# Making the scan's input product on GpSimd a batch ahead, and evicting the first expert block behind the decays

## The chip, the cores and the metric

The kernel runs on one core of a Trainium2 chip. The metric is the device time of one launch in microseconds (us). Inside a core, five engines with a queue of instructions each work side by side and wait for one another through semaphores: TensorE (PE, with its weight loads as PEld), VectorE (DVE), ScalarE (ACT), GpSimd (POOL) and SyncE (SP, which here issues nearly all the transfers). Each engine works through its own queue strictly in order, so that an instruction that waits holds up everything behind it on its engine.

## What is computed

The input is `x` of shape (8, 512, 128): 8 batches of 512 time steps. After a layer norm, a Mamba block `s` and a mixture-of-experts block `g` are computed, and the result is `x + s * g`. The Mamba block is the part that matters here:

```python
x_ssm = silu(conv(x_ssm) + conv_b)
dt = softplus(x_ssm @ dt_w + dt_b)
A = -exp(A_log); Bt = x_ssm @ Bp; Ct = x_ssm @ Cp
def step(state, inp):
    dA = exp(dt_t[:, :, None] * A[None])
    state = state * dA + (dt_t * x_t)[:, :, None] * B_t[:, None, :]
    y_t = einsum('bds,bs->bd', state, C_t)
...
y = (y + x_ssm * D) * silu(z);  s = x + y @ Wout
```

There are 256 channels and 64 states a channel. The product `dt_t * x_t` is what the kernel calls u. The experts (8 routed, of which 2 are chosen for a token, and 2 shared) are matmuls with a gelu between them.

## The kernel before

**Prologue.** For each batch `b` the kernel projects x and z, convolves, makes dt, u, B and C, and stores z (`sz_d`), x (`xs_d`), dt (`dt_d`), u (`u_d`), C (`c_d`) and parts of B. `dt_and_u(b)` on VectorE ends with `dt_new` and `u_new = dt_new * silu_x_new`; `store_dt(b)` on SP stores both, 512 KB each (256 channels of 512 float32). Meanwhile GpSimd sends the normalised tokens to their experts' places in DRAM by 64 indirect stores of 128 rows ("the scatters", line 675), two in flight. Only behind the last of them come its products of the scan phase. Near its end SP starts the scan phase's first loads: rows of C, broadcast to all partitions (`load_c`, 1 MB each), in two halves.

**Scan phase.** Each of 8 batches has 8 groups (`g`) of 8 states, so there are 64 groups, numbered `u = 8 b + g`, and a state step is two scans (`h` = 0, 1, the halves of the channels) over 512 times. In a group the engines do, for state `i`:

- ScalarE makes the decays exp(dt A) in `group_decay` (line 945), a group ahead of VectorE: its decays for group u wait for VectorE's scans of the same state in group u - 1, since they take their place. For kind E it also makes diagonals of B (line 952). Between them stand its evictions: `evict_block(u - 1)` at `i == 4` (line 888, it empties the expert block's bank), `copy_x_block(u)` at `i == 6` (line 894), and behind the eight states `hidden_tiles` with the gelus (lines 905, 913).
- The term u B comes in three kinds, `KIND`. D: PE broadcasts a row of B (line 1435) and VectorE multiplies it by u in PSUM (line 1222). E: PE makes it in `fill` (line 1449) by matmuls of the turned u with a diagonal, in two halves, with expert work between them. P, the last state of the groups with expert blocks: GpSimd multiplies u by a row of B (line 711, at `i == 1`), and ScalarE puts the decay into PSUM (line 939).
- VectorE scans (lines 1240 and 1230), GpSimd multiplies the states by C (line 703, `products`), and PE sums the products (line 1463). States have two buffers: scan `i` waits for product `i - 2`.

The first 40 groups (batches 0 to 4) run an expert block of 256 tokens each (`blocks`); the other 24 gather the experts' rows by indirect loads on GpSimd (line 685, at `i` = 1, 4, 7 of groups 40 to 61) and finish earlier batches (`FINAL_OF`).

In the very first group PE has its expert work late: it turns the tokens at `i == 4`, multiplies at 5 and 6 and at `i == 7` does, in this order, `block_out(0)`, `turn_x(1)` (line 1523), `shared_out(0)` (line 1517), `shared_tile(1)` (line 1512) and a sum, before `group(0, 1)` begins with `fill` for state 1. `turn_x(1)` writes the bank that `evict_block(0)` empties and so waits for it:

```python
def turn_x(m):
    pe.wait_ge(s["x_rows_loaded"], m * 16 + 16)
    pe.wait_ge(s["block_evicted"], m + 1)
```

dt and u of batch b + 1 are loaded in batch b's first group (`load_dt_u`, line 490). x of batch b + 1 for `open_y` (`load_open`, line 480) is loaded at the end of batch b, behind all its groups and ahead of `load_z` and of the next batch's first `load_w1_shared`. Nothing here is reordered by a scheduler: the order on each engine is that of the code.

## Time and profile before

| | us |
|---|---|
| median of 3 runs | 1769.34 (1767.6 to 1770.48) |
| the profiled execution | 1769.54 |
| its span, first to last instruction | 1767.7 |
| VectorE busy | 1617.6 |
| GpSimd busy | 1441.9 |
| DMA, mean over the span | 148 GB/s |

The profile is of one execution. In the timelines a row is a start, a duration, the engine, the line, the instruction and its operands, and how many such instructions in a row were merged; brackets give the idle time ahead of it on its engine and who ended it. Starts are counted from the start of the span. `arena` is the large tile in which most buffers lie, `ps` the PSUM banks.

### The profile page before, as it was taken

The numbers are of one execution on the slowest core, as the hardware profiler recorded it, in microseconds if no ns is written. First come the engines' busy times: TensorE is split into PE (matmuls) and PEld (weight loads), VectorE is DVE, ScalarE is ACT, GpSimd is POOL, SyncE is SP. The second block draws the span as 40 slices with busy tenths as digits, with TensorE's granted clock in tenths as the row PEclk, the third lists the DMA queues.
The fourth block names the chain that finished last, engine by engine and source line by source line (L and its number), as shares of the span: only waits on it lengthen the run. The fifth ranks groups of instructions, "written<-read, shape, count | busy, mean of one in ns | idle before, by whom it ended". The sixth has DMA issues, their size and how long they took to land. (4 is left out here: it accounts for less than half of the span.)

```text
span 1767.7 us, 43328 instructions
## 1 busy us (share of the span) xinstructions
PE 1555.0 (88%) x13334; PEld 802.7 (45%) x13334; DVE 1617.6 (92%) x1818; ACT 1405.0 (79%) x2641; POOL 1441.9 (82%) x716
## 2 busy tenths in 40 slices
PE   5775599999999999999999999988898989999888
PEld 5332344444444444444444444444444444444444
DVE  7888499999999999999999999999998999999987
ACT  4898588788888788877788788788888788888882
POOL 1455588888888888888888888889998899989976
PEclk9897799999999999999999999989999999999999
DMA  8767646676556666675656666555456554655643
GB/s 238 238 220 229 157 119 141 138 162 179 134 136 146 177 146 144 134 186 143 138 135 171 167 139 136 138 143 142 100 132 157 132 131 98 153 141 104 140 80 80
DMA packets 209432, 261.82 MB, mean 148 GB/s; under 512 B 26826, under 2 KB 105428, under 8 KB 209172
## 3 DMA queue, kind: packets, MB, share of 16 engines
q1 hardware_dynamic: 205236, 252.04, 58.9%
q0 software_dynamic: 4096, 8.40, 1.6%
q8 instruction: 69, 1.13, 0.3%
q14 instruction: 31, 0.25, 0.0%
HBM read 216.32 MB, written 43.79 MB: 147 GB/s over the span
## 5 line engine op out<-in xcount | busy, mean ns | idle before, releaser
L703 POOL TENSOR_TENSOR arena<-arena 128x1024 f32<-128x1024 f32 x512 | 1201.5, 2361 | 191.0 <-DVE arena L1240 150.2
L1240 DVE TENSOR_TENSOR_SCAN arena<-arena,ps 128x512 f32<-128x512 f32 x944 | 1085.5, 1203 | 61.0 <-POOL arena L703 38.4
L945 ACT ACTIVATE arena<-arena,neg_A 128x512 f32<-128x512 f32 (+1 forms) x944 | 630.6, 713 | 84.5 <-DVE arena L1240 82.6
L1449 PE MATMUL ps<-arena 128*64 128x128 f32 x6912 | 471.0, 281 | 131.2 <-DVE arena L1240 104.1
L1463 PE MATMUL ps<-arena,ident 64*64 64x512 f32 x4096 | 558.2, 617 | 1.7 <-POOL arena L703 1.6
L1449 PEld LDWEIGHTS ps<-arena 128*64 128x64 f32 x6912 | 375.2, 138 | 364.8 <-DVE arena L1240 190.4
L1222 DVE TENSOR_TENSOR ps<-arena,ps 128x512 f32<-128x512 f32 x512 | 325.2, 681 | 11.2 <-PE ps L1435 11.1
L952 ACT ACTIVATE arena<-ident,b_turned 128x128 f32<-128x128 f32 x864 | 272.9, 387 | 0.0
L1463 PEld LDWEIGHTS ps<-arena,ident 64*64 64x64 f32 x4096 | 107.8, 132 | 181.4 <-issue 174.5
L913 ACT ACTIVATE arena<-ps,arena 128x256 f32<-128x256 f32 x160 | 67.2, 471 | 113.4 <-PE ps L1533 113.4
L675 POOL DMA_INDIRECT x_rms_by_expert<-arena,slots x64 | 71.2, 1112 | 94.9 <-DMA x_rms_by_expert<-arena,slots 60.4
L1230 DVE TENSOR_TENSOR_SCAN arena<-ps,arena 128x512 f32<-128x512 f32 x80 | 93.6, 1211 | 31.8 <-ACT ps L939 31.3
L1435 PEld LDWEIGHTS ps<-b_parts,pick 96*128 96x128 bf16 (+1 forms) x256 | 24.6, 96 | 215.6 <-issue 191.9
L1435 PE MATMUL ps<-b_parts,pick 96*128 96x512 bf16 x256 | 100.1, 391 | 7.8 <-DVEq L1186 6.4
L711 POOL TENSOR_TENSOR arena<-arena 128x1024 f32<-128x1024 f32 x40 | 94.8, 2370 | 0.0
L905 ACT ACT_TABLE_LOAD x64 | 82.1, 1283 | 15.5 <-DVE arena L1230 8.1
L945 ACT ACT_TABLE_LOAD x70 | 89.8, 1283 | 1.2
L1541 PE MATMUL ps<-arena 128*128 128x128 f32 x640 | 89.7, 284 | 0.0
L1541 PEld LDWEIGHTS ps<-arena 128*128 128x128 f32 x640 | 82.5, 195 | 11.8 <-issue 10.7
L1533 PE MATMUL ps<-arena 128*128 128x256 f32 x320 | 86.5, 392 | 0.0
L1517 PE MATMUL ps<-arena 128*128 128x512 f32 x128 | 67.8, 612 | 4.6 <-ACT arena L905 4.4
L1512 PE MATMUL ps<-x_rms,arena 128*128 128x512 f32 x128 | 68.0, 613 | 3.8 <-issue 3.8
(168 smaller groups left out, 1014.0 us busy)
## 6 DMA issues: line engine op xcount, KB each, us to landing
arena<-c_scratch SPq DMA_DIRECT2D x128, 1024.0 KB, 8.5
arena<-w_routed_scaled SPq DMA_DIRECT2D x40, 256.0 KB, 2.8
arena<-in_L_ffn_W_r_dram SPq DMA_DIRECT2D x40, 256.0 KB, 8.8
arena<-c_scratch SPq DMA_DIRECT2D x40, 256.0 KB, 3.3
arena<-w_shared_tiles SPq DMA_DIRECT2D x128, 64.0 KB, 7.8
x_rms_by_expert<-arena SPq DMA_DIRECT2D x1, 5120.0 KB, 27.9
arena<-x_rms_by_expert SPq DMA_DIRECT2D x40, 128.0 KB, 2.4
routed_by_expert<-arena SPq DMA_DIRECT2D x40, 128.0 KB, 8.6
```

The costliest lines, as they stand in the source:

```text
L703: nc.gpsimd.tensor_tensor(products[:, i % RING, :, :], states[:, i % 2, :, :], c_rows[:, i // CG, i % CG, :].unsqueeze(1).broadcast_to((P, ...
L711: nc.gpsimd.tensor_tensor(u_b, u_in.rearrange("p n h t -> p (n h t)")[:, ds(slot, NH * L)].rearrange("p (h t) -> p h t", h=NH), b_row.unsq ...
L945: nc.scalar.activation(decay[:, 2 * i + h, :], dflat[:, ds(slot + h * L, L)], ACT.Exp, scale=aflat[:, ds(col, 1)]).then_inc(s["decay_ready ...
L952: ins = nc.scalar.activation(diag_of(e)[:, c, :], ident[:], ACT.Copy, scale=bt_flat[:, ds(at + c, 1)])
L1222: vector.tensor_tensor(ps[bank][:], uflat[:, ds(slot + h * L, L)], ps[new][:], ALU.mult).then_inc(s["u_b_multiplied"], 1)
L1230: vector.tensor_tensor_scan(states[:, i % 2, h, :], ps[bank][:], u_b[:, h, :], 0.0, ALU.mult, ALU.add).then_inc(s["scanned"], 1)
L1240: vector.tensor_tensor_scan(states[:, i % 2, h, :], decay[:, m, :], ps[bank][:], 0.0, ALU.mult, ALU.add).then_inc(s["scanned"], 1)
L1435: mm(ps[bank][:], pick[:, ds(sel, 1)].broadcast_to((3 * SQ, P)), bflat[:, ds(col, L)], start=True, stop=True).then_inc(s["b_broadcast"], 1)
L1449: ins = mm(bank[HP * r:HP * r + HP, c * P:(c + 1) * P], u_turned[:, odd, c, h * P + HP * r:h * P + HP * r + HP], diag[:, c, :], start=True ...
L1463: ins = mm(y_ps[r][HP * h:HP * h + HP, :], ident[q, q], products[q, slot, h, :], start=False, stop=False, skip_group_check=True)
L1533: mm(bank[:, (RA, RB)[t % 2]], w1_block[:, t, :], x_block, start=True, stop=True, skip_group_check=True).then_inc(s["tile_made"], 1)
L1541: ins = mm(block_ps[:, k * C:(k + 1) * C], hidden_block[:, t, k * P:(k + 1) * P], w2_block[:, t, :], start=(t == 0), stop=(t == HT - 1), s ...
```

## The change

- The prologue makes u and stores it for batch 0 alone. For the others VectorE makes only dt.
- `load_dt_u` loads only dt. GpSimd makes u of batch b + 1 itself in batch b, in group 6 behind the product of state 3 (`make_u`), from the loaded dt and x. The users of u wait for `u_made` in place of the load.
- Since `make_u` needs x, `load_open(b + 1)` moves from the end of batch b to behind group 1's loads.
- In the second group of the kernel (`u == 1`) ScalarE does `evict_block(0)` and `copy_x_block(1)` at `i == 7`, behind the decays, and no longer at 4 and 6. In all other groups they stay.
- GpSimd's and ScalarE's loops over groups are partly written out for it, with a batch 0 of its own.

```diff
@@ SP: load_open, load_dt_u, load_batch, store_dt
-                sp.dma_start(u_d[:, :, b * L:(b + 1) * L].rearrange("h p t -> p h t"), u_new
-                             ).then_inc(s["dt_u_stored"], 16)
+                if b == 0:
+                    sp.dma_start(u_d.rearrange("h p t -> p h t"), u_new).then_inc(s["dt_u_stored"], 16)
...
                 sp.wait_ge(s["sums_opened"], b + 1)
+                if not isinstance(b, int) or b > 1:
+                    sp.wait_ge(s["u_made"], b - 1)
...
-                sp.wait_ge(s["dt_u_loaded"], b * 32 + 32)
-                for dst, src in ((dt_in, dt_d), (u_in, u_d)):
+                sp.wait_ge(s["dt_u_loaded"], b * 16 + 32)
+                flat = dt_in.rearrange("p n h t -> p (n h t)")
...
                 load_group(b, 1, blocks, blocks)
+                if not last:
+                    load_open(b + 1)
...
-                if not last:
-                    load_open(b + 1)
                 load_z(b)
@@ GpSimd
+            def make_u(b, slot):
+
+                pool.wait_ge(s["dt_u_loaded"], b * 16 + 32)
+                pool.wait_ge(s["open_loaded"], b * (16 * N_OPEN) + 16 * N_OPEN)
+                pool.sem_inc(s["u_b_claimed"], 1)
+                part = lambda a: a.rearrange("p n h t -> p (n h t)")[:, ds(slot, NH * L)].rearrange("p (h t) -> p h t", h=NH)
+                nc.gpsimd.tensor_tensor(part(u_in), part(dt_in), silu_x_in, ALU.mult).then_inc(s["u_made"], 1)
...
-                        pool.wait_ge(s["dt_u_loaded"], b * 32 + 32)
+                        if isinstance(b, int) and b == 0:
+                            pool.wait_ge(s["dt_u_loaded"], 32)
+                        else:
+                            pool.wait_ge(s["u_made"], b)
                         pool.wait_ge(s["b_row_loaded"], (b * E + g) * 16 + 16)
+                        pool.sem_inc(s["u_b_claimed"], 1)
...
+                    if isinstance(g, int) and g == E - 2 and i == 3 and not (isinstance(b, int) and b == NB - 1):
+                        make_u(b + 1, next_slot)
@@ ScalarE
+                second = isinstance(u, int) and u == 1
...
-                    if i == 4 and block_before:
+                    if i == (SG - 1 if second else 4) and block_before:
                         evict_block(u - 1)
-                    if i == 6 and block_before and block:
+                    if i == (SG - 1 if second else 6) and block_before and block:
                         copy_x_block(u)
@@ VectorE
-                link(vector.tensor_tensor(dt_new, soft_sum, dt_raw[b % 2], ALU.add))
-                vector.tensor_tensor(u_new, dt_new, silu_x_new[b % 3], ALU.mult).then_inc(s["dt_u_made"], 1)
+                ins = vector.tensor_tensor(dt_new, soft_sum, dt_raw[b % 2], ALU.add)
+                if b == 0:
+
+                    link(ins)
+                    ins = vector.tensor_tensor(u_new, dt_new, silu_x_new[0], ALU.mult)
+                ins.then_inc(s["dt_u_made"], 1)
...
+                    elif i == 0:
+                        dve.wait_ge(s["u_made"], b)
@@ TensorE
-                pe.wait_ge(s["dt_u_loaded"], b * 32 + 32)
+                pe.wait_ge(s["u_made"], b)
```

How it moves instructions is shown at three places. First ScalarE in the kernel's second group, after the change. Line 969 is a decay (945 before), 963 the decay in PSUM (939), 976 a diagonal (952), 912 `evict_block` (888), 918 `copy_x_block` (894) and 929 the gelus' first (905).

```order
164 L969 ACTIVATE arena<-arena,neg_A 128x512 [waits scanned] x6
165 L976 ACTIVATE arena<-ident,b_turned 128x128 x4
166 L969 ACTIVATE arena<-arena,neg_A 128x512 [waits scanned]
167 L963 ACTIVATE ps<-arena,neg_A 128x512 [waits scanned]
168 L969 ACTIVATE arena<-arena,neg_A 128x512
169 L963 ACTIVATE ps<-arena,neg_A 128x512 [waits scanned]
170 L969 ACTIVATE arena<-arena,neg_A 128x512
171 L969 ACTIVATE arena<-arena,neg_A 128x512 [waits scanned]
172 L976 ACTIVATE arena<-ident,b_turned 128x128 x4
173 L912 COPY arena<-ps 128x256 [waits routed_stored,block_made]
174 L918 COPY arena<-ps 128x256 [waits tile_made,x_turned]
175 L929 ACT_TABLE_LOAD [waits w2_used,shared_made,scanned]
```

And the same place before, where the second group is run by the loop.

```order
190 L945 ACTIVATE arena<-arena,neg_A 128x512
191 L979 REGISTER_ALU
192 L945 ISA [waits scanned]
193 L945 ACTIVATE arena<-arena,neg_A 128x512
194 L886 REGISTER_ALU
195 L887 ISA [waits block_made]
196 L888 COPY arena<-ps 128x256 [waits routed_stored]
197 L979 REGISTER_ALU
198 L945 ISA [waits scanned]
199 L945 ACTIVATE arena<-arena,neg_A 128x512
```

The eviction stood ahead of the decays of states 4, 5 and 6; it stands behind them now. The second place is GpSimd in group 6 of batches 1 to 4 after the change: line 712 is a product by C, line 703 is `make_u`.

```order
183 L712 TENSOR_TENSOR arena<-arena 128x1024 [waits scanned]
184 L699 ISA
185 L700 REGISTER_ALU [waits dt_u_loaded]
186 L703 ISA [waits open_loaded]
187 L703 ISA
188 L703 TENSOR_TENSOR arena<-arena 128x1024
189 L710 REGISTER_ALU [waits c_rows_loaded1]
190 L711 REGISTER_ALU [waits y_summed]
191 L712 TENSOR_TENSOR arena<-arena 128x1024 [waits scanned]
```

Before, the products of states 3 and 4 followed each other directly; one more multiplication of the same size stands between them now. The third place is SP at the end of batch 5 and the start of batch 6, before:

```order
290 L440 DMA arena<-xn_scratch 128x512
291 L425 DMA gates_and_ones<-gate_scratch 8x4x128
292 L480 DMA arena<-xs_scratch 128x2x512
293 L503 DMA arena<-sz_scratch 64x2x512 x2
294 L390 DMA arena<-w_shared_tiles 128x128
295 L383 DMA arena<-c_scratch 128x4x512
```

and after the change:

```order
280 L440 DMA arena<-xn_scratch 128x512
281 L425 DMA gates_and_ones<-gate_scratch 8x4x128
282 L504 DMA arena<-sz_scratch 64x2x512 x2
283 L390 DMA arena<-w_shared_tiles 128x128
284 L383 DMA arena<-c_scratch 128x4x512
```

The load of x (512 KB) no longer stands between the loads for finishing a batch and the shared expert's weights of group 48.

## Rows read from the trace of the kernel before

**Rows 1.** The page: busy time of each engine, DMA, and GpSimd's product for kind P.

```profile
PE 1555.0 (88%) x13334; PEld 802.7 (45%) x13334; DVE 1617.6 (92%) x1818; ACT 1405.0 (79%) x2641; POOL 1441.9 (82%) x716
...
DMA packets 209432, 261.82 MB, mean 148 GB/s; under 512 B 26826, under 2 KB 105428, under 8 KB 209172
...
L711 POOL TENSOR_TENSOR arena<-arena 128x1024 f32<-128x1024 f32 x40 | 94.8, 2370 | 0.0
```

**Rows 2.** Waits of VectorE, 230 to 1150 us: total us, times, longest.

```profile
DVE arena L1240 <- POOL arena L703: 12.0, 22, 0.6
```

**Rows 3.** Timeline of VectorE: start us, us, what, idle before.

```profile
193.56 2.33 DVE L1240 TENSOR_TENSOR_SCAN arena<-arena,ps 128x512 f32<-128x512 f32 x2 [10.44 <-POOL arena L703]
...
221.47 1.22 DVE L1230 TENSOR_TENSOR_SCAN arena<-ps,arena 128x512 f32<-128x512 f32 x1 [12.98 <-ACT ps L939]
```

**Rows 4.** Waits of GpSimd, 95 to 148 us.

```profile
POOL x_rms_by_expert L675 <- DMA x_rms_by_expert<-arena,slots: 17.6, 20, 2.6
```

**Rows 5.** Waits of GpSimd, 148 to 192 us.

```profile
POOL x_rms_by_expert L675 <- DMA x_rms_by_expert<-arena,slots: 25.0, 10, 8.5
```

**Rows 6.** Timeline of GpSimd and SP's queue at the end of the scatters.

```profile
176.95 0.80 SPq L383 DMA_DIRECT2D arena<-c_scratch  x1
...
188.91 0.97 POOL L675 DMA_INDIRECT x_rms_by_expert<-arena,slots  x1 [8.49 <-DMA x_rms_by_expert<-arena,slots]
190.19 0.96 POOL L675 DMA_INDIRECT x_rms_by_expert<-arena,slots  x1 [0.30 <-issue]
```

**Rows 7.** Timeline of ScalarE in the second group.

```profile
217.40 0.35 ACT L888 COPY arena<-ps 128x256 f32<-128x256 f32 x1
...
223.99 1.27 ACT L952 ACTIVATE arena<-ident,b_turned 128x128 f32<-128x128 f32 x4
```

**Rows 8.** Timeline of TensorE in the first two groups.

```profile
195.94 1.97 PE L1449 MATMUL ps<-arena 128*64 128x128 f32 x16 [13.57 <-DVE arena L1240]
...
217.89 0.66 PE L1523 MATMUL ps<-ident,arena 128*128 128x128 f32 x2 [4.78 <-ACT arena L888]
...
221.63 1.09 PE L1463 MATMUL ps<-arena,ident 64*64 64x512 f32 x8
224.29 1.09 PE L1449 MATMUL ps<-arena 128*64 128x128 f32 x16 [1.57 <-DVE arena L1230]
...
226.52 1.09 PE L1449 MATMUL ps<-arena 128*64 128x128 f32 x16
```

**Rows 9.** Timeline of VectorE at the same time: scans of states 0 and 1.

```profile
225.25 4.55 DVE L1240 TENSOR_TENSOR_SCAN arena<-arena,ps 128x512 f32<-128x512 f32 x4
```

**Rows 10.** Timeline of GpSimd in group 6 of batch 0.

```profile
353.39 4.70 POOL L703 TENSOR_TENSOR arena<-arena 128x1024 f32<-128x1024 f32 x2
358.39 2.36 POOL L703 TENSOR_TENSOR arena<-arena 128x1024 f32<-128x1024 f32 x1 [0.29 <-DVE arena L1240]
361.81 4.67 POOL L703 TENSOR_TENSOR arena<-arena 128x1024 f32<-128x1024 f32 x2 [1.06 <-DVE arena L1240]
```

**Rows 11.** Timeline of VectorE in group 6 of batch 0.

```profile
359.40 4.55 DVE L1240 TENSOR_TENSOR_SCAN arena<-arena,ps 128x512 f32<-128x512 f32 x4
364.39 2.34 DVE L1230 TENSOR_TENSOR_SCAN arena<-ps,arena 128x512 f32<-128x512 f32 x2 [0.44 <-ACT ps L939]
```

**Rows 12.** Timeline of GpSimd in group 46 (group 6 of batch 5).

```profile
1323.23 4.70 POOL L703 TENSOR_TENSOR arena<-arena 128x1024 f32<-128x1024 f32 x2 [0.83 <-DVE arena L1240]
1328.07 0.99 POOL L685 DMA_INDIRECT arena<-routed_by_expert,slots  x1
1329.06 4.70 POOL L703 TENSOR_TENSOR arena<-arena 128x1024 f32<-128x1024 f32 x2
```

**Rows 13.** Timeline of VectorE in group 46: the last state's scans.

```profile
1331.65 2.33 DVE L1240 TENSOR_TENSOR_SCAN arena<-arena,ps 128x512 f32<-128x512 f32 x2 [0.70 <-POOL arena L703]
```

**Rows 14.** Timelines at the start of batch 6: TensorE, VectorE.

```profile
1361.15 1.84 PE L1512 MATMUL ps<-x_rms,arena 128*128 128x512 f32 x2 [3.77 <-issue]
...
1365.97 2.33 DVE L1240 TENSOR_TENSOR_SCAN arena<-arena,ps 128x512 f32<-128x512 f32 x2 [4.34 <-PE ps L1449]
```

More of the change, by code:

```diff
@@ L721, in group, with run @@
                             gate_attn(FINAL_OF[u])
-            with pool.Fori(0, NB_BLK) as b:
-                slot = pool.snap((b % 2) * (NH * L))
-                with pool.Fori(0, E) as g:
-                    group(b, g, True, slot)
+            def run(b):
+                if isinstance(b, int):
+                    slot, next_slot = (b % 2) * (NH * L), (1 - b % 2) * (NH * L)
+                else:
+                    slot, next_slot = pool.snap((b % 2) * (NH * L)), pool.snap(((b + 1) % 2) * (NH * L))
+                with pool.Fori(0, E - 2) as g:
+                    group(b, g, True, slot)
+                for g in (E - 2, E - 1):
+                    group(b, g, True, slot, next_slot)
+            run(0)
+            with pool.Fori(1, NB_BLK) as b:
+                run(b)
             for b in range(NB_BLK, NB):
                 for g in range(E):
-                    group(b, g, False)
+                    group(b, g, False, None, (1 - b % 2) * (NH * L))
         @block.scalar
```

27 lines of the change are left out of this document (15 added, 12 removed).

## The prediction

> **What bounds the kernel now.** I read four views in this order. The page's busy times name the engine: VectorE is busy for 92% of the span, GpSimd for 82% [rows 1]. VectorE's waits say how little slack the scan phase has: from 230 to 1150 us, which is some 38 groups, its scans waited 12.0 us for GpSimd, 22 times and never over 0.6 us [rows 2]. So in the scan phase any instruction that delays VectorE is paid in full, and GpSimd is the next engine behind it. VectorE's timeline then shows the places where it stands still for long: 10.44 us before 193.56 for GpSimd, and 12.98 us before 221.47 for ScalarE's decays in PSUM [rows 3]. Both hang on one event. GpSimd's first product can only start behind the last scatter, at 191.15 [rows 6], and from there TensorE's late expert work and ScalarE's gelus run in a chain to 221.47. VectorE, ScalarE and TensorE of the prologue had been done some 10 us before, so the prologue ends when the scatters end. GpSimd's own timelines say what its scatters and its products do [rows 4 to 6, 10, 12].
>
> The sum is made against the profiled execution, 1769.54 us (its span is 1767.7); the median of the runs is 1769.34, 0.2 lower.
>
> **1. The prologue: u is not made and not stored seven times.** VectorE loses 7 multiplications. That by itself is worth nothing, since VectorE is already early by its wait of 10.44 us [rows 3]. What can count is what happens to the scatters. A scatter without a wait takes 0.98 + 0.30 = 1.28 us from start to start (188.91 to 190.19 [rows 6]), 64 would need 82 us, and they take until 191.15. The rest is waiting for earlier scatters to land while SP's stores fill the same DMA engines. In 95 to 148 us GpSimd waited 17.6 us in 20 waits [rows 4]; 20 x 0.30 of that is the normal gap, which leaves 11.6. Per batch SP stores z, x, dt and u with 0.50 MB each, B with 0.10 and C with 0.14, 2.24 MB in all, and u is 23% of it. If the excess goes with the bytes in the way, 2.7 us go. In 148 to 192 us it waited 25.0 us in 10 waits [rows 5], an excess of 22; beside three batches' stores there stand 2.25 MB of loads of C and B rows and 0.5 MB of x, and u is 1.5 of some 7 MB, 22%: 4.8 us. Together **-7.5 us**. From below the term is bounded by 0 (the scatters wait for the other stores just as long). From above it is bounded by the whole of the last long wait: without it (8.49 less the normal 0.30 [rows 6]) the scatters would end 8.2 us sooner, and with 2.7 + 3.0 us gained before it (4.8 less the last wait's own 1.8) the gain is about 14.
>
> The scatters are GpSimd's DMAs and meet SP's on the same engines; two of the waits, of over 8 us each, fall behind 1 MB loads of C rows, as the one issued at 176.95 [rows 6]. The Trainium skill, in "DMA: Bandwidth & Descriptors", section "Queues, rings and completion order", says that each DMA engine takes turns between the queues that have work, a packet at a time. By that rule a scatter does not stand behind all the bytes that SP has queued, and taking a third store out would shorten its wait little. The waits of over 8 us speak against it; the ordinary ones of 1 to 3 us don't. What the rule would give is the third rival.
>
> **2. The second group: eviction behind the decays.** Two copies leave the way of the decays that VectorE waits for at 221.47. The one at 217.40 takes 0.35 us, of which I take 0.25 as what holds up the next instruction, since ScalarE's instructions overlap a little; the other is alike. So the two scans of state 7 start 0.25 and 0.5 us earlier. But `turn_x(1)` on TensorE waits for that eviction, and in TensorE's queue behind it stand `shared_out(0)`, `shared_tile(1)`, a sum, and then `fill` for state 1 of the second group, which VectorE needs. Before, the eviction ran at 217.40 and `turn_x(1)` at 217.89, after 4.78 us of waiting [rows 7, 8]. Now the eviction comes behind the diagonal of state 6, which ended at 225.26 and ends 0.5 earlier, 224.75; with its 0.35 us TensorE resumes at 225.2. From there its queue takes what it took before: 217.89 to 222.72 for the four steps (4.83 us), and 224.29 to 227.61 for fill, expert tiles and the second fill (3.32 us) [rows 8]. The second fill is done at 225.2 + 4.83 + 3.32 = 233.35, where it was done at 227.61. VectorE's four scans of states 0 and 1 ran from 225.25 to 229.80 [rows 9]; the last of them can now start at 233.45 and ends at 234.65. That is 4.85 us later. TensorE will also have stood still for 12 us and not 4.8. After 13.57 us of idle time 16 matmuls of a fill took 1.97 us, where they take 1.09 later [rows 8]; if one step more of the queue runs at that speed, it is 0.9 more. I take **+5.3 us**, with bounds 4.0 and 6.5. No earlier waiting hides it, since VectorE is free and waiting there.
>
> **3. `make_u` on GpSimd.** It is a multiplication of 128 x 1024 like the one of line 711, of 2.37 us [rows 1]. It comes seven times, in group 6 of batches 0 to 6. What lies beside other work is GpSimd's idle time behind state 3. In group 6 of batch 0 products 2 and 3 ran to 358.09, product 4 from 358.39 and products 5 and 6 from 361.81 [rows 10]. With `make_u` to 360.43, product 4 ends at 362.76 and product 5 at 365.07, where it ended at 364.15 (361.81 and half of 4.67). VectorE's scan of state 7 needs product 5 and followed it by 0.24 us at 364.39 [rows 11]; the scan of state 6 needs product 4 and moves from 361.68 (359.40 and half of 4.55) to about 362.98, ends at 365.3, and so state 7 starts at 365.31. The loss is 0.92 us, five times: **+4.6 us**. (The decays in PSUM follow state 6's first scan and are done by 365.0; the profile names ScalarE for that wait, but product 5 ends it.) In groups 46 and 54 GpSimd has its gathers instead. In group 46, and I take group 54 as alike, products 3 and 4, the gather and products 5 and 6 run back to back from 1323.23 [rows 12], so nothing is hidden, and the last scan waits for product 5 as it is, 0.70 us [rows 13]: 2.36 us twice, **+4.7 us**. The change also adds a semaphore increment on GpSimd in each of 40 groups. The engines issue such increments between back-to-back work now, and I take 0; it could be the 0.15 us that GpSimd's gathers show as a gap (1327.93 to 1328.07 [rows 12]), 6 us in all.
>
> **4. The moved and removed loads.** At the start of batch 6 TensorE waits 3.77 us for the shared expert's weights, and VectorE then 4.34 us for TensorE [rows 14]. These weights stand in SP's queue behind loads of 1 MB for finishing a batch, 0.52 MB of x and as much of z. At the mean rate of 148 GB/s [rows 1] the 0.52 MB of x take 3.5 us; with loads crowded together the rate is rather higher, so I take **-3.0 us**, with bounds 0 and -4.3, the whole wait. At its new place x stands ahead of a store, of xn and of weights that are used a group later; I cost that, and the loads of u that go, at nothing, and if that cover fails it is at most the same 3.5 us a batch in queue time, and only where the weights are waited for. The wait of `load_open` for `u_made` was met in the batch before.
>
> **The sum:** 1769.54 - 7.5 + 5.3 + 4.6 + 4.7 - 3.0 = 1773.6, and 0.2 less against the median: **1773.5 us**, 0.2% slower.
>
> **The rivals.**
> First, **the scatters get done before the last load of C rows** (not slower). The last two scatters stood behind that load of 176.95 [rows 6]. It decides whether fewer stores bring these two forward by more than the load itself comes forward; if so, none is held up. Term 1 is then -14 and the time 1767.0. Against it: the load's issue follows the last dt, and that comes earlier too, with VectorE's multiplications gone.
> Second, **the eviction costs nothing** (not slower), if ScalarE reaches its eviction much earlier than I place it. Term 2 is then -0.5 and the time 1767.7. Against it: from the eviction's old place to the diagonal's end ScalarE has 7.9 us of work (217.40 to 225.26 [rows 7]), and all of that now stands ahead.
> Third, **the scatters gain little**: only the ordinary waits shrink, term 1 is -2.7, and the time 1778.3.
> Fourth, **GpSimd's extra semaphore instructions show**, 0.15 us in 40 groups, with product 2 behind them on VectorE's path: 1779.5.
>
> **How the numbers follow.** Forecast 0.48, first rival 0.15, second 0.12, third 0.15, fourth 0.10. A measurement of this kernel can tell about 0.2% from no change, which is 3.5 us: slower is from 1772.9 on, faster below 1765.8. The forecast's own spread, mostly that of term 1 (-12 to -3), is 1769 to 1778, of which some 0.6 is above 1772.9. Slower: 0.29 + 0.15 + 0.10 = 0.54. Faster: 0.06 of the first rival, whose own spread reaches there, and 0.04 of the forecast. The same: 0.12 + 0.09 + 0.15 = 0.36. The range leaves out the ends of the first and fourth rivals: 1764.5 to 1780.
>
> **What would show it.** In the profile after: GpSimd's first product at about 183.6 and not 191.16, and the last long wait of the scatters still there; TensorE waiting some 12 us for the eviction in the first group, and VectorE waiting 3 to 5 us for a fill behind its first scans of the second; in group 6 of each of the first five batches a wait of about 1.3 us before state 6's scans, in groups 46 and 54 about 1.9 us and then 0.7 or more; at the start of batch 6 a wait of 1.5 us and not 4.34. I am wrong if the first product moves by more than 12 or less than 3 us, or if VectorE has no wait for the fill.

## The result, and the profile after

The changed kernel takes **1779.05 us** (median of 12 runs, 1777.25 to 1781.59) where the kernel before, run beside it, takes 1770.59 (12 runs, 1766.7 to 1777.66). The ratio is **1.0045, 95% interval 1.0032 to 1.0058**: slower by 5.7 to 10.3 us. The forecast was 1773.5, slower by 4.2.

The profiled executions are 1781.06 us (span 1779.2) after and 1769.54 (span 1767.7) before. They are 11.5 us apart where the medians are 8.5 apart; what is told below from this pair adds up to the 11.5. First the page after, then one line of the list of GpSimd's groups; columns as in [rows 1].

```profile
span 1779.2 us, 43238 instructions
...
PE 1555.6 (87%) x13334; PEld 804.4 (45%) x13334; DVE 1609.5 (90%) x1811; ACT 1406.1 (79%) x2641; POOL 1456.2 (82%) x723
...
DMA packets 205625, 254.48 MB, mean 143 GB/s; under 512 B 26602, under 2 KB 105204, under 8 KB 205364
```

```profile
L703 POOL TENSOR_TENSOR arena<-arena 128x1024 f32 (+1 forms) x7 | 16.6, 2370 | 0.0
```

VectorE is busy 8.1 us less than in [rows 1], and still the kernel is slower: the seven multiplications that it lost stood in the prologue, where it waited. GpSimd is busy 14.3 us more; `make_u` (line 703 now) alone is 16.6, seven times 2.370 us. The traffic fell by 7.34 MB, seven stores and seven loads of u.

**The prologue.** GpSimd and SP at the end of the scatters (start us, us, what, idle before). These rows answer [rows 5, 6].

```profile
POOL x_rms_by_expert L676 <- DMA x_rms_by_expert<-arena,slots: 22.4, 14, 7.2
```

```profile
60.28 1.18 POOL L676 DMA_INDIRECT x_rms_by_expert<-arena,slots  x1 [33.40 <-DVE slots L1204]
...
178.13 0.97 POOL L676 DMA_INDIRECT x_rms_by_expert<-arena,slots  x1 [0.30 <-issue]
182.24 0.97 POOL L676 DMA_INDIRECT x_rms_by_expert<-arena,slots  x1 [3.14 <-DMA x_rms_by_expert<-arena,slots]
188.12 0.96 POOL L676 DMA_INDIRECT x_rms_by_expert<-arena,slots  x1 [4.92 <-DMA x_rms_by_expert<-arena,slots]
...
192.93 4.64 POOL L712 TENSOR_TENSOR arena<-arena 128x1024 f32<-128x1024 f32 x2
```

```profile
177.53 0.38 SPq L383 DMA_DIRECT2D arena<-c_scratch  x1
```

Two rows of before that [rows 6] leave out, for the scatters between the load at 176.95 and the long wait:

```profile
177.06 0.97 POOL L675 DMA_INDIRECT x_rms_by_expert<-arena,slots  x1 [0.30 <-DMA x_rms_by_expert<-arena,slots]
179.46 0.96 POOL L675 DMA_INDIRECT x_rms_by_expert<-arena,slots  x1 [1.43 <-DMA x_rms_by_expert<-arena,slots]
```

The first product starts at 192.93, not earlier than before (191.16) but 1.8 later. The reason is the scatters' start: 60.28 here and 54.09 before, in a stretch that the change doesn't touch. From the first scatter to the first product it is 132.65 us now and was 137.07. I call this the chain of scatters from here on; it is shorter by 4.4.

**The second group.** ScalarE, TensorE and VectorE after (line 912 is `evict_block`, 1559 `turn_x`, 1485 `fill`, 1258 and 1276 VectorE's multiplication and scan); these answer [rows 7 to 9].

```profile
224.71 1.26 ACT L976 ACTIVATE arena<-ident,b_turned 128x128 f32<-128x128 f32 x4
225.88 0.35 ACT L912 COPY arena<-ps 128x256 f32<-128x256 f32 x1
```

```profile
226.37 0.66 PE L1559 MATMUL ps<-ident,arena 128*128 128x128 f32 x2 [12.01 <-ACT arena L912]
226.82 1.92 PE L1553 MATMUL ps<-arena 128*128 128x512 f32 x2
228.53 1.91 PE L1548 MATMUL ps<-x_rms,arena 128*128 128x512 f32 x2
230.38 1.96 PE L1499 MATMUL ps<-arena,ident 64*64 64x512 f32 x8
```

```profile
224.78 1.27 DVE L1258 TENSOR_TENSOR ps<-arena,ps 128x512 f32<-128x512 f32 x2
...
233.41 1.22 DVE L1276 TENSOR_TENSOR_SCAN arena<-arena,ps 128x512 f32<-128x512 f32 x1 [5.12 <-PE ps L1485]
235.49 1.22 DVE L1276 TENSOR_TENSOR_SCAN arena<-arena,ps 128x512 f32<-128x512 f32 x1 [0.86 <-PE ps L1485]
```

TensorE waits 12.01 us for the eviction (4.78 before), the sums behind it take 1.96 instead of 1.09, and VectorE waits 5.12 and 0.86 us for fills where it had no wait. Group 1 lasts 29.89 us, from 224.78 to group 2's first multiplication at 254.67; before it lasted 23.76. Every period below is measured in this way, between the first multiplications (DVE, by rows of B) of two groups.

**`make_u`.** GpSimd and VectorE in group 6 of batch 0, and VectorE in group 46; these answer [rows 10, 11, 13].

```profile
364.99 2.39 POOL L703 TENSOR_TENSOR arena<-arena 128x1024 f32<-128x1024 f32 x1
367.31 4.70 POOL L712 TENSOR_TENSOR arena<-arena 128x1024 f32<-128x1024 f32 x2
```

```profile
369.90 2.33 DVE L1276 TENSOR_TENSOR_SCAN arena<-arena,ps 128x512 f32<-128x512 f32 x2 [1.22 <-POOL arena L712]
```

```profile
1340.05 2.33 DVE L1276 TENSOR_TENSOR_SCAN arena<-arena,ps 128x512 f32<-128x512 f32 x2 [1.71 <-POOL arena L712]
1343.59 2.33 DVE L1276 TENSOR_TENSOR_SCAN arena<-arena,ps 128x512 f32<-128x512 f32 x2 [1.20 <-POOL arena L712]
```

**Batch 6.** TensorE and VectorE after; these answer [rows 14].

```profile
1370.37 1.10 PE L1548 MATMUL ps<-x_rms,arena 128*128 128x512 f32 x2 [1.07 <-issue]
```

```profile
1371.26 4.63 DVE L1276 TENSOR_TENSOR_SCAN arena<-arena,ps 128x512 f32<-128x512 f32 x4
```

VectorE's wait of 4.34 us is gone altogether.

How far the profile after lags behind that of before, in us, at the places between which it changes:

| place | lag | change |
|---|---|---|
| first scatter | 6.2 | 6.2 |
| GpSimd's first product | 1.8 | -4.4 |
| start of group 1 | 0.7 | -1.1 |
| start of group 2 | 6.8 | +6.1 |
| start of the last group | 10.1 | +3.3 |
| end of the span | 11.5 | +1.4 |

The +3.3 are +4.7 for `make_u` in the five batches with expert blocks (groups 6, 14, 22, 30 and 38 are longer by 0.99, 0.87, 0.86, 0.89 and 0.89, group 7 by 0.16), +5.5 in batches 5 and 6 (group 46 +2.31, 54 +1.98, 45 +0.58, 53 +0.68), -3.8 at the start of batch 6, -2.4 at the other six starts of batches together, and -0.8 in groups 57 and 60.

### The profile page after: what moved, and what is told of

Read it like the earlier page. It is cut to its first block and busy times, and to the rows that moved or that the text cites. A ratio compares the mean times of both kernels' runs of the same rounds, so it can differ in the third digit from the quotient of the medians.

```text
span 1779.2 us, 43238 instructions
## 1 busy us (share of the span) xinstructions
PE 1555.6 (87%) x13334; PEld 804.4 (45%) x13334; DVE 1609.5 (90%) x1811; ACT 1406.1 (79%) x2641; POOL 1456.2 (82%) x723
## 3 DMA queue, kind: packets, MB, share of 16 engines
q1 hardware_dynamic: 201428, 244.70, 57.1%
## 5 line engine op out<-in xcount | busy, mean ns | idle before, releaser
L1258 DVE TENSOR_TENSOR ps<-arena,ps 128x512 f32<-128x512 f32 x512 | 325.2, 681 | 10.1 <-PE ps L1471 10.1
L1471 PE MATMUL ps<-b_parts,pick 96*128 96x512 bf16 x256 | 100.2, 391 | 13.1 <-DVE arena L1276 8.5
L686 POOL DMA_INDIRECT arena<-routed_by_expert,slots x64 | 63.2, 987 | 9.6 <-issue 5.3
```

The lines of the kernel that those rows point to most:

```text
L1258: vector.tensor_tensor(ps[bank][:], uflat[:, ds(slot + h * L, L)], ps[new][:], ALU.mult).then_inc(s["u_b_multiplied"], 1)
L1471: mm(ps[bank][:], pick[:, ds(sel, 1)].broadcast_to((3 * SQ, P)), bflat[:, ds(col, L)], start=True, stop=True).then_inc(s["b_broadcast"], 1)
```

## The experiments

Each kernel was timed beside the kernel before, in the same rounds; a gain in us is the ratio's distance from 1 times the median of before. The ratio differs from the quotient of the two medians by up to 0.12% (e9: 1.0001, and 1.0013 by the medians). The medians are of 12 executions, those of e10 and e13 of 6. The last two columns are of the profiled execution: the chain of scatters, and the time from the first product to the start of group 2. One profiled execution can lie far from the median: those of e3, e9 and e11 were the slowest of their twelve (1775.43, 1781.03 and 1775.49 us), those of e10 and e12 the fastest of theirs (1758.13 and 1761.59).

| run | what | median us | before us | ratio, 95% interval | chain | to group 2 |
|---|---|---|---|---|---|---|
| (before) | | | | | 137.1 | 56.7 |
| (after) | | 1779.05 | 1770.59 | 1.0045, 1.0032 to 1.0058 | 132.7 | 61.7 |
| e1 | copies late, alone | 1775.49 | 1771.82 | 1.0025, 1.0011 to 1.0038 | 135.0 | 61.9 |
| e2 | after, copies back | 1771.80 | 1771.82 | 0.9990, 0.9972 to 1.0009 | 125.7 | 57.1 |
| e3 | x loaded early, alone | 1769.59 | 1771.82 | 0.9982, 0.9970 to 0.9994 | 136.5 | 55.9 |
| e9 | after, only copy_x late | 1774.20 | 1771.82 | 1.0001, 0.9984 to 1.0018 | 131.9 | 56.3 |
| e4 | prologue without u | 1767.55 | 1771.03 | 0.9975, 0.9960 to 0.9989 | 131.5 | 56.6 |
| e5 | u made, not stored | 1768.13 | 1771.03 | 0.9984, 0.9968 to 1.0001 | 129.7 | 56.0 |
| e6 | decays in PSUM first | 1771.59 | 1771.03 | 1.0008, 0.9995 to 1.0021 | 135.4 | 55.5 |
| e7 | make_u in quarters | 1765.30 | 1771.03 | 0.9958, 0.9943 to 0.9973 | 133.0 | 55.9 |
| e10 | e7, C rows behind | 1761.10 | 1771.47 | 0.9945, 0.9925 to 0.9965 | 122.3 | 58.5 |
| e11 | before, C rows behind | 1764.52 | 1771.47 | 0.9962, 0.9948 to 0.9977 | 129.9 | 57.5 |
| e12 | e10, x behind too | 1766.85 | 1771.47 | 0.9974, 0.9959 to 0.9989 | 126.5 | 63.3 |
| e13 | e10 again | 1761.64 | 1774.58 | 0.9926, 0.9902 to 0.9951 | 123.7 | 58.2 |

**e1: the two copies moved, in the kernel before.**

```diff
-                    if i == 4 and block_before:
+                    if i == (SG - 1 if second else 4) and block_before:
                         evict_block(u - 1)
-                    if i == 6 and block_before and block:
+                    if i == (SG - 1 if second else 6) and block_before and block:
                         copy_x_block(u)
```

> The kernel before with only the two copies (evict_block(0) and copy_x_block(1)) moved to i == 7 of the second group. My theory: TensorE waits some 12 us for the eviction in place of 4.8, VectorE waits about 5 us for the fill behind its first scans, the period of group 1 goes from 23.76 us to about 29.9 (6.1 more, as after), nothing else moves, and the time is 5.3 to 6.1 us above before. Rival: part of the 6.1 us in the changed kernel came from TensorE or the loads being late behind the changed prologue; then it is clearly less than 5 here.

ScalarE's second group, which ran in the loop, is written out for it. The kernel is slower by 4.4 us (1.9 to 6.7). TensorE's and VectorE's timelines of this kernel show the same two waits as after:

```profile
222.84 0.66 PE L1526 MATMUL ps<-ident,arena 128*128 128x128 f32 x2 [12.01 <-ACT arena L888]
```

```profile
229.93 1.22 DVE L1243 TENSOR_TENSOR_SCAN arena<-arena,ps 128x512 f32<-128x512 f32 x1 [5.18 <-PE ps L1452]
```

Group 1 lasts 29.94 us. That is the edit's whole effect: the other parts of the change have no share in it.

**e2: the changed kernel with both copies back at 4 and 6.**

```diff
-                    if i == (SG - 1 if second else 4) and block_before:
+                    if i == 4 and block_before:
...
-                    if i == (SG - 1 if second else 6) and block_before and block:
+                    if i == 6 and block_before and block:
```

> The changed kernel with the two copies back at i == 4 and 6 in the second group. My theory: the costs are additive, so it is 6 us below after, about 1773, 2 to 3 us above before: make_u +10.2, products' start and loads -7 or so. Rival (the eviction is hidden by another wait of the second group): within 2 us of after, 1777 or more.

Group 1 lasts 23.76 us again, and the kernel can't be told from the kernel before (0.9990). The loss of the change thus sits in the eviction; the rest about cancels. This profile also shows something that the experiment was not made for. GpSimd's and SP's timelines:

```profile
176.46 0.97 POOL L676 DMA_INDIRECT x_rms_by_expert<-arena,slots  x1 [0.30 <-issue]
180.69 0.97 POOL L676 DMA_INDIRECT x_rms_by_expert<-arena,slots  x1 [3.27 <-DMA x_rms_by_expert<-arena,slots]
181.68 4.67 POOL L712 TENSOR_TENSOR arena<-arena 128x1024 f32<-128x1024 f32 x2
```

```profile
175.87 0.38 SPq L383 DMA_DIRECT2D arena<-c_scratch  x1
```

The load of C rows is issued at 175.87, and only two scatters start behind it. Each scatter waits for the one two before it to land, since two are in flight. In every profile with the load in its old place, the first scatter that starts behind the load is a slow one: before, that of 177.06 landed at 188.65, just ahead of the load itself (188.89), and the scatter of 188.91 had to wait for it. In e2 this first one, of 176.46, is the last but one of all, so no scatter waits for it; only the 3.27 us are left, and the chain is 125.7 us. That is the prediction's first rival, in the same prologue that took 132.7 in the profile after.

**e9: only copy_x_block late.** The first half of the same edit: `evict_block(0)` stands at 4 again, `copy_x_block(1)` at 7.

```diff
-                    if i == (SG - 1 if second else 4) and block_before:
+                    if i == 4 and block_before:
```

> The changed kernel with evict_block(0) back at i == 4 of the second group and only copy_x_block(1) left at i == 7. My theory: the loss comes from turn_x(1) waiting for evict_block(0) alone, so this is within 1 us of the kernel with both copies back, about 1773, and VectorE's wait of 5 us for the fill is gone. Rival: the expert tiles of group 1 wait for copy_x_block(1) and delay the fills as much; then it stays near 1779.

It can't be told from before (1.0001). TensorE waits 4.78 us for the eviction, as before, and 0.18 us for the other copy:

```profile
216.12 0.66 PE L1559 MATMUL ps<-ident,arena 128*128 128x128 f32 x2 [4.78 <-ACT arena L912]
...
223.53 1.13 PE L1569 MATMUL ps<-arena 128*128 128x256 f32 x4 [0.18 <-ACT arena L918]
```

So `evict_block(0)` alone makes the loss, through `turn_x(1)`.

**e3: load_open early, in the kernel before.**

```diff
                 load_group(b, 1, blocks, blocks)
+                if not last:
+                    load_open(b + 1)
...
-                if not last:
-                    load_open(b + 1)
                 load_z(b)
```

> The kernel before with only load_open(b + 1) moved ahead, to behind group 1's loads. My theory: the wait at the start of batch 6 goes from 4.34 us to about 1, the period of that group falls by 3.8, the other starts of batches move by 2 us or less either way, and the time falls by 3 to 4 us. Rival: the gain at batch 6 comes from u no longer being loaded there (0.52 MB less in the queue), then the wait stays at 4 us and the time does not move.

Measured: 3.2 us faster (1.1 to 5.3), as expected, while the profile shows hardly anything of it: group 48, expected 3.8 us shorter, lasts 31.5 us for 31.6 before. TensorE and VectorE at the start of batch 6:

```profile
1363.84 2.04 PE L1512 MATMUL ps<-x_rms,arena 128*128 128x512 f32 x2 [2.31 <-issue]
...
1367.73 3.17 PE L1449 MATMUL ps<-arena 128*64 128x128 f32 x32
```

```profile
1369.75 2.42 DVE L1240 TENSOR_TENSOR_SCAN arena<-arena,ps 128x512 f32<-128x512 f32 x2 [3.93 <-PE ps L1449]
```

TensorE waits 2.31 us for the weights instead of 3.77, and then its fill takes 3.17 us where it took 1.97. The granted clock there is 0.60 in this profile and 1.00 in the profile of before, so what the weights gain is lost again in this one execution. Over all profiles, group 48 lasts 31.5, 31.6, 33.6, 33.9, 34.2 and 34.5 us in the six with the late load, mean 33.2; it lasts 27.9, 28.3, 28.4, 28.5, 29.4, 29.7 and 30.0 in the seven with the early load and without loads of u, mean 28.9. With the early load alone it is 31.5, once. The whole edit is worth 4.3 us there. How it divides between x and u, one profile doesn't settle (the slowest of its twelve executions at that), though the time of e3 speaks for x.

**e4 and e5: the prologue alone.** In e4 VectorE makes no u behind batch 0 and SP stores none; in e5 VectorE makes it and only the store goes. In both the scan phase loads dt in u's place, so u is wrong in batches 1 to 7 and the loads weigh the same.

```diff
-                sp.dma_start(u_d[:, :, b * L:(b + 1) * L].rearrange("h p t -> p h t"), u_new
-                             ).then_inc(s["dt_u_stored"], 16)
+                if b == 0:
+                    sp.dma_start(u_d[:, :, b * L:(b + 1) * L].rearrange("h p t -> p h t"), u_new
+                                 ).then_inc(s["dt_u_stored"], 16)
...
-                for dst, src in ((dt_in, dt_d), (u_in, u_d)):
+                for dst, src in ((dt_in, dt_d), (u_in, dt_d)):
```

and in e4 besides:

```diff
-                vector.tensor_tensor(u_new, dt_new, silu_x_new[b % 3], ALU.mult).then_inc(s["dt_u_made"], 1)
+                if b == 0:
+                    link(ins)
+                    ins = vector.tensor_tensor(u_new, dt_new, silu_x_new[0], ALU.mult)
+                ins.then_inc(s["dt_u_made"], 1)
```

> The kernel before, whose prologue neither makes nor stores u of batches 1 to 7; the scan phase loads dt of the same size in u's place (so u is wrong there, and the loads weigh the same). This is the prologue's part of the change alone. My theory by the sum: the chain from the first scatter to GpSimd's first product takes 137.1 us less 7.5 or so and the time is 7 us below before. Rival (the scatters gain little): the chain falls by no more than 3 us, and the time by 1 to 3 us. The changed kernels so far had chains of 132.7, 131.9 and 125.7 us, those with the prologue of before 137.1, 136.5 and 135.0, so I expect 126 to 133 and a time 5 us below before.

> The same, but VectorE still makes u of every batch and only the store is left out (u in the scan phase is dt again). My theory: it is the bytes of the store in the scatters' way that count, so the chain of scatters and the time are as without the multiplications, within 2 us. Rival: VectorE's 7 multiplications set when dt and what hangs on it are ready, then the chain and the time stay at those of before.

e4 is faster by 4.4 us (1.9 to 7.1), e5 by 2.8 (-0.2 to 5.7). The chains are 131.5 and 129.7 us. The two agree within their intervals, and both chains are shorter than any of the old prologue, so it is the store that held the scatters up; VectorE's multiplications did nothing that shows. (By its time alone e5 can't quite be told from before.) Together with after, e2, e9 and e7, six profiles have the changed prologue and the load of C rows in its place; their chains have a mean of 130.8 us. The four with the old prologue (before, e1, e3, e6) have 136.0. The stores are worth **5.2 us** in the mean, and 4.2 without e2, whose chain is shorter for the reason given above; the five others are all between 129.7 and 133.0, the four old ones between 135.0 and 137.1.

**e6: the decays in PSUM first.** [rows 3] show VectorE waiting 12.98 us for two decays in PSUM that stand behind a group's work on ScalarE. This kernel is the one before with these two put first in the second group (written out, as in e1), and the copies earlier among the decays.

```diff
+                if second:
+                    for h in range(NH):
+                        act.wait_ge(s["scanned"], m0 + (2 * (P_AT - 2 + h) + (2 - h)))
+                        decay_to_psum(*before, h)
...
-                    if i == 4 and block_before:
+                    if i == (1 if second else 4) and block_before:
-                    if i == 6 and block_before and block:
+                    if i == (3 if second else 6) and block_before and block:
```

> The kernel before with ScalarE's work of the second group in another order: the two decays in PSUM first, ahead of the group's other decays, then evict_block(0) at i == 1 and copy_x_block(1) at i == 3. If VectorE's wait of 12.98 us before state 7's scans of the first group is for the decays in PSUM and for nothing else late, these scans start 9 us sooner and group 1 starts sooner by that; group 1's own decays then come later and give some of it back: the time falls by 6 us. Rival: GpSimd's product of state 5 or TensorE ends that wait next, and the time falls by less than 2 us.

It can't be told from before (1.0008). VectorE and TensorE in the second group:

```profile
210.75 2.34 DVE L1237 TENSOR_TENSOR_SCAN arena<-ps,arena 128x512 f32<-128x512 f32 x2 [3.59 <-ACT ps L939]
...
231.35 1.29 DVE L1229 TENSOR_TENSOR ps<-arena,ps 128x512 f32<-128x512 f32 x2 [7.21 <-PE ps L1442]
```

```profile
225.93 2.08 PE L1540 MATMUL ps<-arena 128*128 128x256 f32 x4 [5.45 <-ACT arena L905]
```

The wait of 12.98 us became 3.59, and group 1 starts 23.1 us behind the first product instead of 32.9. But group 1 then lasts 32.42 us instead of 23.76. Its expert tiles need the gelu (line 905) that stands behind all of ScalarE's decays, and that starts at 223.89 where it started at 225.28 (the first product was 1.3 earlier as well): from the first group's last gelu, at 207.78, to there ScalarE is busy without a break. My expectation named the wrong rival: neither GpSimd nor TensorE came next, but ScalarE's own queue, one group later. From that gelu on the wait was time that ScalarE lacked, and this other order of its queue didn't give it.

**e7: make_u in quarters.** The changed kernel with the copies back, and `make_u` cut into four multiplications of 128 x 256, each in another place.

```diff
+                    at = {(E - 3, 4): 0, (E - 3, 7): 1, (E - 2, 4): 2, (E - 2, 7): 3} if blocks else \
+                        {(E - 5, 2): 0, (E - 4, 2): 1, (E - 3, 2): 2, (E - 2, 2): 3}
-                    if isinstance(g, int) and g == E - 2 and i == 3 and not (isinstance(b, int) and b == NB - 1):
-                        make_u(b + 1, next_slot)
+                    if isinstance(g, int) and (g, i) in at and not (isinstance(b, int) and b == NB - 1):
+                        make_u(b + 1, next_slot, at[g, i])
```

> The changed kernel with the copies back at i == 4 and 6 and make_u cut into four multiplications of 128 x 256, each placed alone (groups 5 and 6 at i == 4 and 7 in the block batches; groups 3 to 6 at i == 2 in the others). My theory: a piece of some 0.6 us fits into GpSimd's idle time of a group, so the 0.9 us in each of five groups 6 and the 2 us in groups 46 and 54 go, and the time is 8 us below the kernel with make_u whole and copies back, some 6 to 8 us below before. Rival: GpSimd's idle time in a group is made up of pieces too short, each quarter is paid with its gap (0.6 us or more), 28 quarters cost 15 us and it is slower than with make_u whole.

It is **7.4 us faster than before** (4.8 to 10.1). GpSimd's timeline in group 5 of batch 0:

```profile
333.36 2.36 POOL L715 TENSOR_TENSOR arena<-arena 128x1024 f32<-128x1024 f32 x1 [0.39 <-DVE arena L1281]
335.67 0.74 POOL L704 TENSOR_TENSOR arena<-arena 128x256 f32<-128x256 f32 x1
336.75 4.68 POOL L715 TENSOR_TENSOR arena<-arena 128x1024 f32<-128x1024 f32 x2 [0.34 <-DVE arena L1281]
```

Behind the quarter GpSimd still waits 0.34 us for VectorE: the piece lies wholly in idle time. Groups 14, 22, 30, 38, 46 and 54 last as long as in the kernel before, within 0.02 us; groups 44 and 53 are 0.24 longer, and groups 5 to 7 of batch 0 0.15 each. So of the 9 to 10 us that `make_u` cost whole, about 1 is left, though four quarters take 4 x 0.74 = 2.96 us against 2.37.

**e11, e10 and e13: the race with the C rows.** The prologue's last load of C rows is issued when all scatters have landed, in the kernel before (e11) and in that with quarters (e10, and e13 once more).

```diff
-                if p == NB + 1:
-                    load_c(0, 0, 1, 0)
...
                 sp.wait_ge(s[f"x_sorted{n}"], 16 * TOPK * NT // IN_FLIGHT)
+            load_c(0, 0, 1, 0)
             load_x_rows(0)
```

> The kernel before with only that: the last load of C rows issued when all scatters have landed. My theory: the wait of 8.49 us goes, the scatters end 5 to 8 us sooner, and so does everything behind; with C rows needed some 11.5 us behind the first product and 6 to 8.5 us on their way it costs nothing: 5 us below before. Rival: with u's stores there the scatters are held up by these instead, or product 4 waits for the rows: within 1 us of before.

> The kernel with make_u in quarters and the copies at i == 4 and 6, and besides the prologue's last load of C rows (1 MB, half 1 of group 0) issued only when all scatters have landed. In the one changed kernel whose scatters were done when that load came, their chain took 125.7 us; in the others, with 3 to 5 scatters behind it, 129.7 to 133.0. My theory: that race is the first rival of the prediction, and held back the load always loses it; the chain takes 122 to 127 us, the load lands before GpSimd's product of state 4 needs it, and the time is 4 to 6 us below the kernel with quarters alone, some 11 us below before. Rival: the scatters wait for the last stores just as long, or product 4 now waits for C rows, and the time does not move.

> The kernel with make_u in quarters and the last C rows behind the scatters once more, since only half of its runs could be used and whether the race is always won rests on one profile. My theory: the chain of the scatters takes 122 to 127 us whatever the start, and the time is 9 to 12 us below before. Rival: the first look was lucky, the chain is back at 130 us or more and the time no better than with the quarters alone, 7 us below before.

e11 is faster than before by 6.7 us (4.1 to 9.2); e10 by 9.7 (6.2 to 13.3) and e13, the same kernel, by 13.1 (8.7 to 17.4). GpSimd's and SP's timelines of e10:

```profile
178.80 0.97 POOL L675 DMA_INDIRECT x_rms_by_expert<-arena,slots  x1 [1.26 <-DMA x_rms_by_expert<-arena,slots]
...
181.06 4.66 POOL L714 TENSOR_TENSOR arena<-arena 128x1024 f32<-128x1024 f32 x2
...
193.95 4.67 POOL L714 TENSOR_TENSOR arena<-arena 128x1024 f32<-128x1024 f32 x2 [1.31 <-DMA arena<-c_scratch]
```

```profile
182.54 0.39 SPq L383 DMA_DIRECT2D arena<-c_scratch  x1
```

The long wait is gone, and the chain is 122.3 and 123.7 us, where six profiles of the changed prologue with the load in its old place show 125.7 to 133.0. The old prologue goes from 136.0 to 129.9. The price is that GpSimd waits 1.31 us for the C rows and that the stretch up to group 2 is some 2.5 us longer than in e7; what is left is a gain. The medians of e10 and e13, 1761.1 and 1761.6, are the lowest of all kernels, but e7 was not timed beside them, so their lead over e7 rests on the ratios (0.9945 and 0.9926 against 0.9958), whose intervals overlap.

**e12: x of batch 0 behind the scatters too.**

```diff
-            load_open(0)
...
             load_c(0, 0, 1, 0)
             load_x_rows(0)
+            load_open(0)
```

> As with quarters and the C rows behind the scatters, and the load of x for batch 0 (0.52 MB) behind them too. My theory: with the C rows gone the scatters no longer stand behind much, so this gives 0 to 1 us more. Rival: whatever bytes SP queues there hold the last scatters up, then it gives 2 us more, or TensorE waits for x and it costs some.

It is 4.6 us faster than before, less than e10 (the intervals just overlap), where 0 to 1 us more was expected. TensorE's timeline shows what it lost:

```profile
191.98 1.98 PE L1449 MATMUL ps<-arena,diagD 64*64 64x512 f32 x8 [6.15 <-DMA arena<-xs_scratch]
```

x was issued at 181.5 and took 10.4 us among the loads around it; TensorE waits 6.15 us for it and VectorE 6.40 us for TensorE. The chain (126.5 us) is no shorter either. Holding a load back helps only if nobody needs it soon.

## Why the prediction was right or wrong

Its direction and its places were right; its size was not: 4.2 us slower was forecast and 8.0 measured (5.7 to 10.3), and the median is 5.6 us above the forecast, near the end of its range. Point by point:

**The reading of the kernel** held. VectorE's seven multiplications are gone, and its 8.1 us less of busy time bought nothing, as said. The price is paid where VectorE waits for one event in the first two groups and for GpSimd later.

**Term 1, the scatters: -7.5 forecast, -5.2 measured** (the mean of ten chains; -4.4 in the pair of profiles, and -4.4 by the time of e4, 1.9 to 7.1). This is the term that was mis-sized, and the step that failed is the one behind 148 us. The first step, that the excess goes with the bytes in the way, was to give 2.7 of the 7.5 before 148 us. The pair of profiles doesn't show it (GpSimd waited 17.6 us there before [rows 4] and 18.4 after, with a scatter start 6 us later), but the ten do: a mean of 18.8 us in the four with the old prologue and 16.5 in the six with the new, 2.3 less. From 148 to 192 us the same share of 22% was to give 4.8. It gave 2.6 in the pair (25.0 [rows 5] and 22.4) and 3.4 in the ten (24.2 and 20.8).

The waits behind the loads of C rows don't shrink by that share. The one behind the load issued at 148 to 155 us has a mean of 7.6 us in the four old profiles and 7.1 in five of the new (all but e2). That behind the last load, with the shorter wait just ahead of it (1.43 + 8.49 before, 3.14 + 4.92 after, 2.99 + 5.38 in e7), has 9.5 and 8.3. Nor were the last two scatters alone behind that load, as I had read it, and e10's expectation miscounts them too: four to seven start behind its issue in the old profiles (four before), three to six in the five new ones, two in e2. The wait is about the same whatever their number, since it stands for the first of them. Only where this one is among the last two of all, as in e2, do most of the 8.3 us go.

So the term has two values for one and the same prologue, -4.2 (five profiles) and -10.3 (one), and the first rival and the forecast can both come true. Which one comes is a matter of when the load is issued within the chain. The sign that I gave, a first product at 183.6, did not come in any kernel with the load in its place but e2, which came even earlier; and by my own bound I was wrong as soon as the product moved by less than 3 us. It moved by +1.8. I had compared clock times, though, and not the chain: the scatters' start alone varies from 52.6 to 60.3 us over 14 profiles.

**Term 2, the eviction: +5.3 forecast, +5.5 measured.** From the first product to group 2 it is 61.7 and 61.9 us with the late eviction (after and e1), and 56.35 in the mean of the six with it in its place and the C rows too (before, e2, e3, e4, e5, e7). Each step came as worked out: the eviction ended at 226.2 (forecast 225.1, with all else 1.8 late), TensorE waited 12.01 us, the second fill's scan waited. The increment for a slow TensorE was right to be there: the sums behind the wait took 1.96 us and not 1.09. The second rival fell with e1.

**Term 3, `make_u`: +4.6 and +4.7 forecast, +4.7 and +4.2 measured.** The five block groups lost 0.86 to 0.99 each, for 0.92. VectorE waited 1.22 us before state 6's scans (some 1.3 forecast), and the 0.44 before state 7's [rows 11] are gone. In group 46 its two waits are 1.71 and 1.20 (forecast 1.9, then 0.7 or more). Groups 46 and 54 lost 2.31 and 1.98 after, 2.30 and 1.85 in e2, and 2.32 and 3.29 in e9. Whether the two steps of 0.6 to 0.7 us in groups 45 and 53 belong to the term stays open: e2 has neither, e9 has that of group 53, and e1, which has no `make_u`, has such steps in groups 50, 51 and 59.

**The fourth rival, semaphore increments,** fell. Groups 2 to 5 last 23.76 us before and 23.76 to 23.77 after.

**Term 4, batch 6: -3.0 forecast, -4.3 measured** in the mean of profiles (-3.8 in the pair). The gain is larger than forecast and at its bound, the whole wait of 4.34 us. TensorE's wait for the weights fell from 3.77 to 1.07 us in the pair, 2.7 less for the 3.0 forecast. What I left out is the work behind the wait: before, at a granted clock of 0.54, the matmuls with the weights and the sums took 1.84 and 1.99 us; after, at 1.00, they take 1.10 and 1.09.

**The third rival** (the scatters gain 2.7 at most; 1778.3) has the time nearest to the one measured, but its reason is not borne out. The chains differ by 5.2 us, or 4.2 without e2, where it allows 2.7, and in e11 the chain is 6.1 us shorter with only that one 1 MB load out of the way. (The times of e4 and e5 alone, with -4.4 and -2.8, don't rule 2.7 out.) The Trainium skill, in "DMA: Bandwidth & Descriptors", section "Queues, rings and completion order", states the turns per packet and adds that a packet may hold many descriptors; no run here shows how many of the load's go in one turn. What the rows show is that the scatter of 177.06 before, 0.1 us behind the load, landed at 188.65, about when the load did: that was 11.9 us on its way from 176.95.

**The sum.** With the measured terms it is -5.2 + 5.5 + 8.9 - 4.3 = +4.9 us. The other kernels fit sums of this kind: without the late eviction -0.6 (e2 measured -1.8, from -5.0 to 1.6), and with the quarters' 1 us in place of 8.9 it is -8.5 (e7 measured -7.4, from -10.1 to -4.8). The changed kernel itself measured +8.0, from 5.7 to 10.3. The 5.5 agree with e1's own time, +4.4 (1.9 to 6.7). Some 1 to 5 us of the 8.0 are not explained by any term. A candidate is the scatters' start: it is 52.6 to 60.3 with the changed prologue (nine profiles, mean 57.7) and 54.1 to 58.7 with the old one (five, mean 56.1). With such a spread the 1.6 us can't be told from chance, and I leave it open.

## What to carry to other kernels

Moving work off the busiest engine pays only where that engine is not waiting, and the engine that takes it must have idle time in pieces as long as the work: the same multiplication cost 0.9 to 2.3 us whole and next to nothing in quarters. Before an eviction is moved behind other work, follow who waits for its bank, and everything queued behind that waiter; 0.5 us was to be gained for one engine, and 5.5 were lost through another. Where small transfers in a chain share the DMA engines with a large load that is not yet needed, try holding the load back until the chain is done, but no longer than its first reader allows.

## What the runs showed of the hardware

- **Small indirect stores wait for a large load that was issued ahead of them.** With two stores of 128 rows of 512 B in flight, a chain of them waits 3.1 + 4.9, 3.0 + 5.4 or 1.4 + 8.5 us behind a load of 1 MB, and mostly 0.6 to 3.5 us a wait behind the ordinary stores. Of six profiles with the same changed prologue and the load in its old place one, e2, had only 3.3 us of it, so executions that differ in nothing at this place can be some 6 us apart in the chain. The chain's start varies by 7.7 us over the 14 profiles.
- **The same wait is followed by different clocks.** At the start of batch 1 TensorE idles 2.11 us in both before and e1. Its next fill takes 1.09 us in the one, at a granted clock of 1.00, and 1.97 in the other, at 0.51, that is at the lower of its two levels, 1.2 and not 2.4 GHz. The period of that group is 24.91 or 26.14 us accordingly, and the starts of batches 1 to 4 take either value from profile to profile. TensorE's timeline and the engines' busy time in that stretch (us, busy of PE, PEld, DVE, ACT and POOL, granted clock, DMA share, GB/s), of before and then of e1:

```profile
399.60 1.09 PE L1449 MATMUL ps<-arena 128*64 128x128 f32 x16 [2.11 <-DVE arena L1240]
```

```profile
399.50:402.00 2.50, 2.32 (x25) 1.27 (x26) 2.50 (x6) 2.50 (x8) 2.50 (x2) 1.00 0.56 161
```

```profile
402.94 1.97 PE L1452 MATMUL ps<-arena 128*64 128x128 f32 x16 [2.11 <-DVE arena L1243]
```

```profile
402.90:405.40 2.50, 2.46 (x20) 1.88 (x24) 2.50 (x5) 2.50 (x8) 2.50 (x2) 0.51 0.61 171
```

- **A quarter of a GpSimd multiplication takes 0.74 us,** where a quarter of 2.37 would be 0.59: by a straight line through the two, an estimate, some 0.2 us are fixed.
